# Two stacked attention layers: another order for the loads and splits ahead of the first units

## The reference

```python
def layer(x, ...):                       # both layers, cut to what they share
    xn = layernorm(x, g_in)
    q = xn @ Wq                          # 512 -> 1024
    k, v = split(xn @ Wkv)               # 512 -> 2 x 64
    k, v = concat([null_k, k]), concat([null_v, v])
    sim = einsum('bhid,bjd->bhij', q, k) + bias      # scaled; layer 1 normalises q and k
    attn = softmax(where(causal_mask | padding_mask, neg, sim))
    out = einsum('bhij,bjd->bhid', attn, v) @ Wo     # 1024 -> 512
    return layernorm(out, g_out)

# bias of layer 1, for n = 128 positions
h = silu(ln(pos @ w0 + b0, g0))          # first layer of the chain
h = silu(ln(h @ w1 + b1, g1))            # second layer, 512 x 512
bias = (h @ w2 + b2)[i - j + n - 1]      # 512 x 16

x = x + layer0(x); x = x + layer1(x)
```

## Time and profile before

| | |
|---|---|
| median of 3 runs | 2378.75 us (2378.54 to 2379.0) |
| profiled execution | 2378.64 us, span 2376.8 us, granted TensorE clock 0.994 |
| busy share of the span | PE 98%, DVE 68%, ACT 67%, POOL 38% |
| chain that ended last | PE 95%, then ACT, DMA, DVE and SP's queue at 1% each |

### The profile page before, as it was taken

One profiled execution on the slowest core, in us unless ns is written; L12 is line 12 of the kernel. 1 busy time (PEld: TensorE's weight loads), 2 busy tenths in 40 slices (PEclk: granted clock), 3 DMA queues, 4 the chain that ended last, 5 costly groups with the idle time before them and its releaser, 6 DMA issues.

```text
span 2376.8 us, 55129 instructions
## 1 busy us (share of the span) xinstructions
PE 2326.9 (98%) x17435; PEld 2040.4 (86%) x17435; DVE 1604.6 (68%) x4513; ACT 1596.3 (67%) x6497; POOL 911.8 (38%) x1699
## 2 busy tenths in 40 slices
PE   4899999999999999999999999999999999999998
PEld 4788888888888888888888888888888888888877
DVE  5667667667667667676666676676676676666666
ACT  3767666667666666666677666676666666666666
POOL 2334334433433433443343343343334334334432
PEclk8999999999999999999999999999999999999999
DMA  7111111111121111111111111111111111211111
GB/s 242 40 49 46 48 61 43 51 54 44 52 61 43 48 56 47 52 55 45 52 54 40 61 48 48 56 45 48 61 43 48 56 46 52 61 43 48 57 38 38
DMA packets 108116, 129.50 MB, mean 54 GB/s; under 512 B 46305, under 2 KB 50465, under 8 KB 108081
## 3 DMA queue, kind: packets, MB, share of 16 engines
q1 hardware_dynamic: 105952, 127.70, 17.6%
q10 hardware_dynamic: 1776, 1.32, 0.2%
q0 software_dynamic: 352, 0.05, 0.1%
HBM read 81.79 MB, written 33.57 MB: 49 GB/s over the span
## 4 chain that ended last, share of the span: by engine, by line
PE 95%; ACT 1%; DMA 1%; DVE 1%; SPq 1%; issue 0%; POOL 0%; POOLq 0%; DVEq 0%
PE psum L711 30%; PE psum L607 17%; PE psum L575 15%; PE psum L663 10%; PE psum L697 10%; PE psum L674 6%; PE psum L537 3%; PE psum L624 2%; PE psum L586 2%; DMA w_raw<-in_L_cond_Wkv_dram 1%; ACT probs L868 0%; SPq L389 0%; DMA k_high<-kv_t 0%; PE psum L615 0%; PE psum L594 0%
## 5 line engine op out<-in xcount | busy, mean ns | idle before, releaser
L1359 POOL TENSOR_TENSOR weights<-probs,den_inv 128x256 f32<-128x256 f32 (+3 forms) x1024 | 473.9, 490 | 1411.9 <-DVE den_inv L1094 1407.7
L868 ACT ACTIVATE probs<-probs,neg_max 128x129 f32<-128x129 f32 (+3 forms) x2048 | 716.0, 352 | 311.0 <-DVE neg_max L1088 310.9
L1081 DVE TENSOR_TENSOR probs<-psum,masked_bias 128x324 f32<-128x324 f32 x512 | 225.7, 483 | 272.9 <-PE psum L663 271.9
L1346 POOL TENSOR_TENSOR masked_bias<-bias,pad_neg 128x516 f32<-128x516 f32 (+3 forms) x512 | 397.0, 808 | 13.4 <-POOL pad_neg L1342 4.4
L868 ACT ACTIVATION_READ_ACCUMULATOR probs<-probs,neg_max 128x1 f32 x2048 | 385.6, 188 | 0.0
L711 PE MATMUL psum<-wo_hi,o_hi 128*128 128x512 f32 x1024 | 272.0, 407 | 0.8 <-issue 0.8
L711 PE MATMUL psum<-wo_hi,o_lo 128*128 128x512 f32 x1024 | 267.5, 403 | 1.0 <-DVE o_lo L1099 1.0
L1088 DVE TENSOR_REDUCE neg_max<-probs 128x2 f32<-128x258 f32 (+3 forms) x1024 | 257.0, 313 | 4.5
L711 PE MATMUL psum<-wo_lo,o_hi 128*128 128x512 f32 x1024 | 259.4, 395 | 0.0
L875 ACT COPY probs_t<-psum 128x384 f32<-128x384 f32 (+1 forms) x512 | 192.5, 429 | 74.1 <-PE psum L674 73.9
L711 PEld LDWEIGHTS psum<-wo_lo,o_hi 128*128 128x128 f32 x1024 | 192.2, 188 | 46.6
(11 more groups left out here) (136 smaller groups left out, 4373.7 us busy)
## 6 DMA issues: line engine op xcount, KB each, us to landing
res<-in_x_dram SPq DMA_DIRECT2D x64, 256.0 KB, 2.7
x_of<-y_out SPq DMA_DIRECT2D x64, 256.0 KB, 2.1
res<-x_of SPq DMA_DIRECT2D x64, 256.0 KB, 2.7
out_dram<-y_out SPq DMA_DIRECT2D x64, 256.0 KB, 2.1
xa<-in_x_dram SPq DMA_DIRECT2D x63, 256.0 KB, 2.7
xa<-x_of SPq DMA_DIRECT2D x63, 256.0 KB, 2.8
q_aside<-qp SPq DMA_DIRECT2D x32, 256.0 KB, 2.8
w_raw<-in_L_cond_Wq_dram SPq DMA_DIRECT2D x8, 512.0 KB, 8.7
```

Of the source, the lines that this page charges most:

```text
L868: x_ = nc.scalar.activation(s, s, ACT.Exp, bias=neg_max[:, g, k, e:e + 1], accum_out=den[:, g, k, e:e + 1])
L1081: a = nc.vector.tensor_tensor(probs[:, 2 * c + e, :], SB[c][e][:, 0:ROW], masked_bias[:, 2 * c + e, :], ALU.add)
L1346: m = nc.gpsimd.tensor_tensor(block(masked_bias, b), block(bias[u.layer], b), pad_neg[u.layer][:, 0:WIDTH[b]].unsqueeze(1).to_broadcast([P ...
L1359: m = nc.gpsimd.tensor_tensor(places[b], block(pairs(probs, g // 2), b)[:, :, 1:1 + n], den_inv[:, g, k, :].unsqueeze(2).to_broadcast([P, ...
```

## The change

Only the start is touched.

SP loads three rows of the bias network and the 16 transfers of the given bias right behind pieces 0 to 3, then the masks, the third input row, the other two rows, `null_v` and the residual; then it waits for and issues the two copies (`put_aside`, `copy_keys`), and all later weights come behind them. The bias network's weights (`w1_loads`) are issued by GpSimd, once piece 3 has landed.

On ScalarE and VectorE the two input rows are normalised and split ahead of all parts of the weights. The first layer of the bias chain comes right behind the four low parts; the null key and null biases come behind it. The parts of Wo (pieces 4 to 7) are split later: the high parts at the end of `begin`, the low parts in `first0` between the unit's own steps.

On TensorE the first tile of the projection no longer waits for all low parts: its products take each piece as its high part is done, then the low inputs, then the low parts one by one. The other tiles are as before.

```diff
@@ SP, begin @@
                 load_pieces(range(KC))
+                start(sp, rows_loads[:3], rows_loaded[0])
+                start(sp, rest_loads, rest_loaded)
                 for k in range(2):
                     sp.dma_start(keep[k][:, :], row((keep0, keep1)[k][0], S)).then_inc(keep_loaded[k], 16)
+                load_xa(n)
+                start(sp, rows_loads[3:], rows_loaded[1])
                 start(sp, [(null_v[:, :], row(null_kv[1], DH))], null_v_loaded)
-                start(sp, w1_loads, w1_loaded)
-                load_xa(n)
-                start(sp, rest_loads, rest_loaded)
                 load_res(w.even)
+                put_aside(w)
+                copy_keys(w)
                 load_pieces(range(KC, 2 * KC))
                 start(sp, g_out_loads, g_out_loaded)
                 load_xa(n2)
-                load_pieces(range(2 * KC, 3 * KC))
-                put_aside(w)
-                copy_keys(w)
-                load_pieces(range(3 * KC, 4 * KC))
+                load_pieces(range(2 * KC, 4 * KC))
                 load_keep_behind(then)
                 copy_pair_v(w)
@@ PE, project_pair @@
-                    for xs, ws in ((xp_hi, w_hi), (xp_hi, w_lo), (xp_lo, w_hi)):
-                        if h == 0 and t == 0 and n != KC:
+                    arriving = u is None and h == 0 and t == 0
+                    hi_lo, lo_hi = (xp_hi, w_lo), (xp_lo, w_hi)
+                    for xs, ws in ((xp_hi, w_hi), lo_hi, hi_lo) if arriving else ((xp_hi, w_hi), hi_lo, lo_hi):
+                        if h == 0 and t == 0 and ws is w_hi:
                             wait(pe, x_hi_done if n == 0 else x_lo_done, w.odd.xdone)
                         for c in range(KC):
+                            if arriving and n // KC != 1:
+                                wait(pe, hi_done if n < KC else lo_done, c + 1)
@@ PE, begin @@
                 transpose_odd(w)
-                pe.wait_ge(lo_done, KC)
                 project_pair(w, 0, (0, 1, 2, 3), None)
@@ ACT, begin @@
                 start(act, gain_loads, gain_loaded)
-                start(act, rows_loads[:3], rows_loaded[0])
-                start(act, rows_loads[3:], rows_loaded[1])
                 act.wait_ge(consts_done, 2)
                 rstd_of_input(w.even)
+                split_x(w.even)
+                rstd_of_input(w.odd)
+                split_x(w.odd)
                 act.wait_ge(gain_loaded, 16 * len(gain_loads))
-                high_parts((0, 1))
-                split_x(w.even)
-                high_parts((2,))
-                rstd_of_input(w.odd)
-                high_parts((3,))
-                split_x(w.odd)
-                rstd_of_input(n)
+                high_parts(range(KC))
                 rstd_of_h(0)
                 sigmoid(0)
                 for k in range(2):
                     take_half(w, 0, k)
-                high_parts(range(KC, 2 * KC))
                 null_norm()
+                rstd_of_input(n)
                 for k in range(2):
                     take_half(w, 1, k)
+                high_parts(range(KC, 2 * KC))
@@ DVE, first0 @@
                 split_x(w.odd)
+                low_parts((KC,))
                 silu(1)
-                inverse_sum(u, (2, 3))
+                inverse_sum(u, (2,))
+                low_parts((KC + 1,))
+                inverse_sum(u, (3,))
+                low_parts((KC + 2,))
+                silu_transposed(1)
+                low_parts((KC + 3,))
+                last_layer()
                 low_parts((2 * KC,))
-                silu_transposed(1)
-                last_layer()
+                diagonals_transposed()
                 low_parts((2 * KC + 1,))
-                diagonals_transposed()
@@ POOL, ahead of its stages @@
+            pool.wait_ge(raw_loaded[KC - 1], 32)
+            start(pool, w1_loads, w1_loaded)
```

More of the change, by code:

```diff
@@ L1220, in begin @@
                 normalise(w.even)
-                low_parts((0, 1))
+                input_statistics(w.odd)
                 split_x(w.even)
-                input_statistics(w.odd)
                 normalise(w.odd)
-                low_parts((2, 3))
                 split_x(w.odd)
-                input_statistics(n)
-                normalise(n)
-                null_key()
-                place_null_biases()
+                low_parts(range(KC))
                 first_layer()
@@ L1233, in begin @@
                 silu(0)
-                low_parts((KC,))
+                null_key()
+                place_null_biases()
                 silu_transposed(0)
+                take_kvt(w)
+                null_key_scaled()
+                input_statistics(n)
+                normalise(n)
+                second_layer()
                 dve.wait_ge(null_v_loaded, 16)
-                take_kvt(w)
-                low_parts(range(KC + 1, 2 * KC))
-                null_key_scaled()
-                second_layer()
                 take_pair_v(w)
```

## The result

The changed kernel takes 2375.5 us (median of 20 runs, 2372.45 to 2377.62), the kernel before 2378.64 us in the same comparison (20 runs, 2375.42 to 2382.19). The ratio is 0.9984, with a 95% interval from 0.9978 to 0.999: 3.1 us faster where 10.5 were forecast, and outside the range of 2363.5 to 2373.5. The profiled execution took 2376.46 us (span 2374.7).

What follows compares the result with a forecast made beforehand. TensorE's standstills in the first 60 us bound the kernel, then the late keep row: 11.4 us earlier at product(1) less 0.9 for the clock gives 10.5, 2378.64 - 10.5 = 2368.1 us; range 2363.5 to 2373.5.

Steps and rivals of the forecast that it cites:

- What bounds the kernel: First 60 us: TensorE stands still 32 us, waiting 12.9 for second row's xn, 1.5 low part, 4.7 h, 4.3 copied keys.
- Keys: Copied keys and fourth input row: k_high issued at 28.6, the 4.3 us wait gone, add_bias at 42.0, next projection 13.4 earlier.
- The late keep row: Second unit's mask row lands at 52.3, POOL waits 4 us as new bound; product(1) at 58.5, 11.4 earlier.
- Edits at nothing: Low parts of Wo in first0 cost nothing, hidden in DVE's idle time; up to 4.9 us if that cover were gone.
- Clock: Ahead of product(1): a 2.3 us PE standstill may bring slow clock, 0 or 1.7 us lost; half taken, 0.9.
- The sum: At product(1) 11.4 - 0.9 = 10.5 us earlier, the same work in the same order behind it; 2368.1 us.
- The rules: w1 on POOL's queue: descriptors locked out by DVE, 3.5 us to spare; or rows slowed by shared queues, 1.2 us, 2369.3.
- (c): w1 comes late from POOL, landing at 40, and holds product(0) until 43.6; 2370.9 us, chance 0.08.
- (d): Slower: w1 on POOL's queue ends with the run of weights, at 52; 2383.7 us, chance 0.04.
- (b): Piece 3 of the weights lands no earlier than before, at 18 to 19; gain 7, 2371.6 us, chance 0.13.
- (a): The keep row lands in time, by 48 to 50, gain 14.3; 2364.3 us, chance 0.20.
- (e): Inputs' split is late because ACT or DVE waits for something ahead of it; 2378.6 us as before, chance 0.05.

Runs made afterwards that it cites:

- e3: Changed kernel with residual, second mask, two bias-network rows and null_v issued later on SP, for a shorter list ahead of the copies; 2374.95 us, ratio 0.9987 to the kernel before.
- e1: Changed kernel with the second unit's keep row asked for right behind the two copies, ahead of all later weights; 2371.81 us, ratio 0.9975 to the kernel before.
- a0: The changed kernel run once more without edits, also called the repeat, as base for the other runs; 2376.5 us, ratio 0.9989 to the kernel before.
- e4: Changed kernel with the four low parts of Wo back at the end of VectorE's begin, not in first0; 2368.53 us, ratio 0.9966 to the kernel before.
- e6: Changed kernel with the keep row ahead of all later weights and the low parts of Wo back in begin; 2370.13 us, ratio 0.9967 to the kernel before.
- e10: Changed kernel with low parts of Wo back in begin and without TensorE's late wait for all low parts; 2368.31 us, ratio 0.9954 to the kernel before.
- e8: Kernel before with only the four low parts of Wo moved from begin to first0; 2381.79 us, ratio 1.0014 to the kernel before.
- e5: Changed kernel without TensorE's wait for all low parts ahead of the loop's first unit; 2370.8 us, ratio 0.9972 to the kernel before.
- e7: Changed kernel with third and fourth input rows and keep row asked for earlier, Wo parts split in first0, no late wait; 2359.4 us, ratio 0.9921 to the kernel before.
- e2: Changed kernel with 24 unread transposes on PE in the standstill ahead of the first unit's last two probability transposes; 2371.34 us, ratio 0.9968 to the kernel before.
- e9: The version with the input rows first (2359.4 us) plus unread identity transposes in five TensorE standstills; 2361.99 us, ratio 0.9927 to the kernel before.

## Why the prediction was wrong, step by step

**What bounds the kernel, the inputs first, the weights, the first projection, the bias chain: right.** Second row's high part 10.94 (forecast 11.0), piece 3 there at 15.06 (15.0), transposes of h at 25.52 (25.7), `product(0)` over at 35.2 (35.5).

**Keys: right in the mechanism, 2.7 to 2.9 us too early in size.** The 16 biases took 15.82 us to issue where the earlier trace rows gave 11.12. They now stand right behind the pieces and three rows; that this is the reason was not tested. `k_high` went out at 31.33 instead of 28.6 and the first Wo at 31.97 instead of 29.1. So the fourth row landed at 43.7 (35.59 + 8.1) and not at 41.1, `add_bias` started at 44.50 and not at 42.0, and the projection came 10.6 earlier, not 13.4. e3 shows that a shorter list gives back 0.7 to 1.0 of it at `add_bias`.

**The late keep row: right as a mechanism** (POOL waited 4.64, forecast 4), and 3.0 us mis-sized: it landed at 55.3 instead of 52.3 (44.82 + 10.5). e1 shows its price as long as the mask is slow: 3.3 us by the ratios, 1.2 at the second unit's scores.

**Edits at nothing: this is the step that failed.** It called the low parts of Wo in `first0` free, on DVE's idle time in the earlier trace rows, and bounded them by DVE's own time. They cost no time on DVE's chain. They cost it on POOL, whose mask was by the forecast's own account the new bound, and through POOL's delay on TensorE's clock. The start of the second unit's scores in four kernels that differ in two edits alone:

| | low parts in `first0` | low parts back in `begin` |
|---|---|---|
| `keep` row behind all pieces | 69.94 (a0) | 65.68 (e4) |
| `keep` row early | 68.74 (e1) | 63.90 (e6) |

The forecast amounts to 63.85 (74.35 - 10.5), with the row late. The low parts are worth 4.3 and 4.8 us here, and of the 4.3 only 1.1 lie ahead of `product(1)`; the rest is the clock behind it, 4.40 us to the scores instead of 7.56. One more kernel with the row late and the low parts back, e10, has a part of the slow clock (5.95 us) and its scores at 67.02, so 2.9 is the low end. In the whole time e4 gives 5.5 us by the ratios. Its profiled execution gains 8.4, of which up to 4 may be luck, by the stretch behind 110 us and the one near the end. e8 costs 3.3 us in the kernel before. So the same step shows from both sides. With e4's median of 2368.53 or e6's of 2370.13 the stated range would have held.

The Trainium skill has the rule, SBUF — State Buffer, "SBUF: two separate sides": a VectorE operation with two inputs in SBUF and a GpSimd operation that reads SBUF hold one pair of ports by turns, each for a whole instruction. The traces agree in that both engines lose (2.03 against 1.22 us, 5.52 against 3.53), and the operation that starts first, the low part at 55.61 in the changed kernel, isn't slowed (1.20). A smaller case stands in the kernel before: `h<-h,sig` of the bias chain (L1162), also with two inputs in SBUF, takes 0.95 us beside the mask of 3.53, and 0.69 in e4, where the mask begins behind it and takes 3.09. The prediction read that section for w1 alone.

**Clock: right that a standstill ahead of `product(1)` brings slow clock, mis-sized.** Forecast 2.3 us of standstill and 0.9 lost; it was 3.21 and 2.9 (7.0 ahead at `product(1)`, 4.1 at the scores). The forecast tied the slow clock to a standstill of 2.3 us; in e1 and e8 it follows standstills of 0.9 and 1.15 us too. A second stretch, behind the standstill of 2.83 us at 113, had been left as it was; it grew, and took 1.6 more (4.3 to 2.7). e5 shows that this standstill and its slow clock were worth 4.0. The prediction's sum has no change there, since it took all behind `product(1)` to run as before.

**The sum**, at the second unit's scores: 10.5 forecast, less 3.0 for the row, 1.3 for the mask and 2.0 for the clock is 4.2; measured 4.1. Of these 4.1, 2.7 are left behind the slow stretch at 115 us and 2.1 at the end of the span; the medians differ by 3.1.

**The rules and rivals.** w1 from POOL's queue landed in 6.2 us beside a busy DVE, so neither rule on it had a price here, and rivals (c) and (d) didn't happen. Nor did (b), as piece 3 was there at 15.06. (a) was refuted by the wait for `keep`, and (e) by the second row's transposes at 9.24.

Left open: what decides whether a slow clock follows a standstill, and for how long. It followed 0.9 and 1.15 us (e1, e8), not 1.23 (e4), in part 1.49 (e10), and 2.28 us near the end in some executions and not in others. So executions of one kernel lie some us apart: e4's five from 2368.08 to 2372.24, the 20 of the kernel before from 2375.42 to 2382.19.

## What to carry to other kernels

Before work on an engine is called hidden, look at who shares its ports at that moment: idle time on VectorE is no cover if GpSimd stands on the critical path beside it. When a chain moves forward, the next bound can be a small transfer at the end of a long list; here it was worth more to move that one entry (3.3 us) than to shorten the list (0.5). Count a standstill of TensorE with what the clock takes behind it, and give that term both ends. And follow a gain through the trace to the end: a difference of 2 or 3 us between two kernels can come from a place that neither edit touches.

## What the runs showed of the hardware

- VectorE and GpSimd slow each other: four low parts of 1.22 us beside a mask and a division took 2.03, 1.70, 1.41 and 1.27, and the two GpSimd steps 9.2 us instead of 5.4. Free of DVE's two-input work the mask takes 3.07 to 3.09 us (e4, e6).
- A standstill of 3.2 us was followed by stretches near half the clock (0.56 and 0.58) that cost about as much again (2.9 us). The same work, from `product(1)` to the second unit's scores, took 4.4 us in e4, e6 and e7 and 7.6 in the repeat, e1 and e8, in the last two behind standstills of 0.9 and 1.15 us. Unread matmuls in a standstill helped in one place (e2) and not in another (e9).
- The same standstill of 2.28 us near the end was followed by a clock of 0.53 in one execution and 1.00 in another, 2.5 us apart.
- The `keep` row of 16 KB, behind 12 pieces of weights, took 10.5 us from its issue to landing; in e7, ahead of them, 4.2. Issuing took longer where the list was more crowded ahead: 16 biases 15.82 us instead of 11.12.
- GpSimd's queue moved 1 MB in 6.2 us while the biases were loading and VectorE was busy, where SP's queue beside other loads had taken 12.6.
